# The second expert layer of a two-layer model: three row buffers, the choice of experts one batch sooner, and its biases as one rounded matmul pass over 24 rows

## The reference, cut to what matters

```
scores = maximum((x @ gate_W + gate_b) / 1.0, 1e-4)
p = softmax(scores)
_, topk_idx = top_k(p, 2)
topk_mask = one_hot(topk_idx, 8).sum(-2) > 0
w = maximum(p, 0.1)
w = w / take_along_axis(w, topk_idx).sum(-1)
comb = where(topk_mask, w, 0)
y = einsum('bsd,edf->bsef', x, expert_W) + expert_b
out = einsum('bsef,bse->bsf', y, comb) / 2
```

## Time and profile before

| what | us |
|---|---|
| median of 3 runs (2248.28 to 2251.6) | 2251.52 |
| span of the profiled execution, first to last instruction | 2243.7 |
| start of the last stage's first load | 1951.0 |
| first and last batch's first bias matmul | 1980.35 and 2211.24 |

### The profile page before, as it was taken

One profiled execution on the slowest core, in us unless ns is written; L12 is line 12 of the kernel. 1 busy time (PEld: TensorE's weight loads), 2 busy tenths in 40 slices (PEclk: granted clock), 3 DMA queues, 4 the chain that ended last, 5 costly groups with the idle time before them and its releaser, 6 DMA issues. The chain is left out here.

```text
span 2243.7 us, 32891 instructions
## 1 busy us (share of the span) xinstructions
PE 1923.3 (86%) x9910; PEld 1128.5 (50%) x9910; DVE 1660.0 (74%) x2326; ACT 1242.8 (55%) x2642; POOL 1427.3 (64%) x1164
## 2 busy tenths in 40 slices
PE   2499999999873999956899999999999996579998
PEld 1244444444432999953345454544444442267676
DVE  4478888787734756520999999999999999546554
ACT  1066666676652434326786868686868575223232
POOL 7334445543343444431999999999999999534344
PEclk9789999999875999977999999999999999879899
DMA  3544544444144444421231314040404040200110
GB/s 79 107 98 104 114 106 109 115 110 123 50 154 132 92 72 76 77 45 61 110 123 47 135 36 157 13 161 10 161 10 151 10 158 3 67 11 29 37 37 19
DMA packets 231218, 185.60 MB, mean 83 GB/s; under 512 B 148729, under 2 KB 201601, under 8 KB 231058
## 3 DMA queue, kind: packets, MB, share of 16 engines
q1 hardware_dynamic: 216178, 162.61, 25.1%
q0 software_dynamic: 13296, 17.77, 4.4%
q10 hardware_dynamic: 1584, 3.24, 0.5%
HBM read 134.07 MB, written 49.49 MB: 82 GB/s over the span
## 5 line engine op out<-in xcount | busy, mean ns | idle before, releaser
L1780 POOL TENSOR_TENSOR mb_dbu<-mb_dtu,mb_bbc 128x1024 f32<-128x1024 f32 x256 | 598.6, 2360 | 5.2 <-DVE mb_da_ps L1937 2.4
L473 ACT ACTIVATE ex_plain<-at_t_ps 128x512 f32<-128x512 f32 x512 | 289.4, 595 | 176.1 <-PE at_t_ps L851 170.2
L1937 DVE TENSOR_TENSOR_SCAN mb_da_ps<-mb_da_ps,mb_dbu 128x1024 f32<-128x1024 f32 x160 | 365.3, 2283 | 4.0 <-ACT mb_da_ps L1830 3.3
L1972 PE MATMUL mb_y_ps<-mb_hc,lw_ident 128*128 128x512 f32 x640 | 312.3, 611 | 44.9 <-DVE mb_hc L1944 44.4
L610 DVE TENSOR_REDUCE at_mx<-at_s_ps 128x2 f32<-128x1024 f32 x256 | 310.8, 1218 | 48.3 <-PE at_s_ps L860 45.3
L860 PE MATMUL at_s_ps<-ex_w 48*128 48x512 f32 x512 | 226.1, 503 | 37.5 <-DVE at_mx L610 24.1
L851 PE MATMUL at_t_ps<-ex_w 64*128 64x512 f32 x512 | 219.8, 485 | 12.4 <-ACT ex_plain L473 7.1
L1786 POOL TENSOR_TENSOR mb_hp<-mb_hp,mb_cbc 128x1024 f32<-128x1024 f32 x96 | 226.0, 2354 | 0.0
L1935 DVE TENSOR_TENSOR_SCAN mb_hp<-mb_da_ps,mb_dbu 128x1024 f32<-128x1024 f32 x96 | 218.8, 2280 | 6.5 <-POOL mb_dbu L1780 5.5
L1211 POOL DMA_INDIRECT x<-m_o,m_xs x71 | 113.7, 1601 | 172.7 <-DMA x<-m_o,m_xs 106.3
L1972 PEld LDWEIGHTS mb_y_ps<-mb_hc,lw_ident 128*128 128x128 f32 x640 | 117.7, 192 | 203.7 <-issue 124.5
(11 more groups left out here) (322 smaller groups left out, 4148.1 us busy)
## 6 DMA issues: line engine op xcount, KB each, us to landing
mb_bbc<-mb_scr SPq DMA_DIRECT2D x64, 512.0 KB, 6.2
mb_cbc<-mb_scr SPq DMA_DIRECT2D x64, 512.0 KB, 6.2
ex_w<-at_scr SPq DMA_DIRECT2D x384, 64.0 KB, 2.3
m_xs<-rt_rows SPq DMA_DIRECT2D x71, 129.0 KB, 2.0
at_scr<-at_qk_hi SPq DMA_DIRECT2D x32, 256.0 KB
at_scr<-at_qk_lo SPq DMA_DIRECT2D x32, 256.0 KB
at_xin<-in_x SPq DMA_DIRECT2D x32, 128.0 KB, 2.2
ex_plain<-in_x SPq DMA_DIRECT2D x8, 512.0 KB
```

The costliest lines, as they stand in the source:

```text
L473: act.activation(probs[:, c, h, :], t_ps[:, k % 2, :], ACT.Exp, scale=SCALE).then_inc(exp_done, 1)
L1780: pool.tensor_tensor(dbu[:, q % 3, :, :], dtu_2, bbc[:, 2 * p:2 * p + 2, :], ALU.mult).then_inc(S["dbu_ready"], 1)
L1937: dve.tensor_tensor_scan(da, da, add, 0.0, ALU.mult, ALU.add).then_inc(S["scan_done"], 1)
L1972: last = pe.matmul(y_ps[:, v % 2, :], ident[:, :], src[:, j, :], start=False, stop=(q == tile_last[v] and j == 1))
```

## The change

The four tables of places and the loop over two batches are gone; the eight batches are written out. Rows have three buffers instead of two, so that a batch's rows are there two batches ahead. Variance (and ACT's root) of batch n + 2 is taken at the end of batch n; the other steps for batch n + 1 move forward: normalising after unit 0, turned rows after 3, gate after 6, and on DVE scores after 6, the first choice after 8, the second after 10, the shares after 12. PE turns the shares after unit 14. DVE's instructions for the choice are the same as before.

The bias product becomes one pass of rounded numbers: the shares are split into a rounded part and the rest, and stand three times beside each other (`comb_3`: rounded, rest, rounded) against biases that stand three times below each other (`eb_3`: rounded, rounded, rest), 24 rows in all. This adds three small DVE instructions per batch, and in the prologue four on the biases and one more constant, `parts_of`.

```
-        x = sb("x", [P, 2, 4, D])
+        x = sb("x", [P, XB, 4, D])
...
-        combT = sb("combT", [E, 2, T])
+        comb_3 = sb("comb_3", [P, 4, 3, E], F32R)
+        combT = sb("combT", [3 * E, 2, T], F32R)
...
+                for n in range(NB):
+                    for u in range(UNITS):
+                        if u % 2:
+                            add_odd(n, u)
+                        if u == 7 and n + 1 < NB:
+                            low(n + 1)
...
+                            if u == 3:
+                                take_rows(n + 1)
+                            if u == 7:
+                                exponents(n + 1)
+                            if u == 14:
+                                take_comb(n + 1)
+                        if u == 15 and n + 2 < NB:
+                            root(n + 2)
...
+                    dve.tensor_scalar(comb[:, n % 2, :, :], m1, 0.5, None, ALU.mult).then_inc(S["comb_ready"], 1)
+                    dve.wait_ge(S["comb_ready"], n + 1)
+                    wait(dve, S["combT_ps"], n)
+                    top_steps(dve.tensor_copy(comb_3[:, :, 0, :], comb[:, n % 2, :, :]))
+                    dve.tensor_copy(comb_3[:, :, 2, :], comb_3[:, :, 0, :])
+                    dve.tensor_tensor(comb_3[:, :, 1, :], comb[:, n % 2, :, :], comb_3[:, :, 0, :], ALU.subtract).then_inc(S["comb_3_ready"], 1)
...
+                    for u in range(0, UNITS, 2):
+                        accumulate(n, u)
+                        if n + 1 < NB:
+                            if u == 0:
+                                normalise(n + 1)
+                            if u == 6:
+                                scores(n + 1)
+                            if u == 8:
+                                first_choice(n + 1)
+                            if u == 10:
+                                second_choice(n + 1)
+                            if u == 12:
+                                shares(n + 1)
+                        if u == 14 and n + 2 < NB:
+                            variance(n + 2)
...
+                    wait(pe, S["b_added"], 2 * n + k // 2 - 1)
+                    pe.wait_ge(S["eb_ready"], 4)
+                    for a in range(2):
+                        last = pe.matmul(b_ps[:, k // 2, a * D:(a + 1) * D], combT[:, n % 2, (k + a) * P:(k + a + 1) * P], eb_3[:, :], start=True, stop=True)
...
+                        if n + 1 < NB:
+                            if u == 3:
+                                turn_rows(n + 1)
+                            if u == 6:
+                                gate(n + 1)
+                            if u == 14:
+                                turn_comb(n + 1)
```

More of the change, by code:

```diff
@@ L1439, in _ @@
                 act.preload_act_table_set("natural_log_exp_and_others")
[L1440 to L1464, removed]
@@ L1466, in weigh_odd, with root @@
[L1466 removed]
+                act.wait_ge(S["const_set"], 1)
+                def root(n):
+                    act.wait_ge(S["var_ready"], n + 1)
+                    wait(act, S["xn_ready"], n)
+                    act.activation(rs[:, 0, :], mv[:, :, 1], ACT.Ln, bias=eps[:, :]).then_inc(S["ln_ready"], 1)
+                    act.wait_ge(S["ln_ready"], n + 1)
+                    act.activation(rs[:, 0, :], rs[:, 0, :], ACT.Exp, scale=-0.5).then_inc(S["rs_ready"], 1)
@@ L1496, in slot @@
+                root(0)
+                upper(0)
+                upper(1)
+                take_rows(0)
+                root(1)
+                exponents(0)
+                upper(2)
+                upper(3)
+                take_comb(0)
+                for n in range(NB):
+                    act.wait_ge(S["comb_ready"], n + 1)
                     for u in range(UNITS):
                         if u % 2:
-                            weigh_odd(n, b, u)
-                        if following and u in ACT_AT:
-                            before(*following, ACT_AT.index(u))
@@ new lines, in gate, with turn_comb @@
+                def gate(n):
+                    pe.wait_ge(S["xT_hi_ready"], n + 1)
+                    for k in range(4):
+                        for kt in range(2):
+                            last = pe.matmul(f_ps[:, 0, k * E:(k + 1) * E], xT[:, kt, k * P:(k + 1) * P], gw[:, kt, :], start=(kt == 0), stop=(kt == 1))
+                    last.then_inc(S["logits"], 1)
+                def turn_comb(n):
+                    pe.wait_ge(S["comb_3_ready"], n + 1)
+                    for k in range(4):
+                        last = pe.transpose(f_ps[0:3 * E, 0, k * P:(k + 1) * P], comb_3[:, k, :, :].rearrange("p s e -> p (s e)").bitcast(F32), ident[:, :])
+                    last.then_inc(S["combT_ps"], 1)
@@ new lines, in biases @@
+                def biases(n, k):
+                    wait(pe, S["b_added"], 2 * n + k // 2 - 1)
+                    pe.wait_ge(S["eb_ready"], 4)
+                    for a in range(2):
+                        last = pe.matmul(b_ps[:, k // 2, a * D:(a + 1) * D], combT[:, n % 2, (k + a) * P:(k + a + 1) * P], eb_3[:, :], start=True, stop=True)
+                    last.then_inc(S["b_ready"], 1)
+                turn_rows(0)
+                gate(0)
+                turn_comb(0)
+                for n in range(NB):
+                    pe.wait_ge(S["xT_lo_ready"], n + 1)
+                    pe.wait_ge(S["combT_ready"], n + 1)
```

333 lines of the change are left out of this document (157 added, 176 removed).

## The result

The changed kernel takes 2231.56 us (median of 4 runs, 2228.57 to 2237.41) against 2251.56 for the kernel before: a ratio of 0.992, interval 0.9901 to 0.9939. It is faster, as forecast.

The account below looks back on a forecast made before the run. PE in the last stage was taken to bound the kernel, 33.0 us a batch. Seven batches -12.6, the last -1.5, prologue +3.9 gave -10.2, so 2241.3 us; own range 2235 to 2248, over all cases 2228 to 2254.

Parts of the forecast that it names:

- The waits: PE's stalls per batch: 0.9 for normalised rows after unit 3, 2.7 for shares after unit 14; the shares' copy wait goes.
- The price of `xT_lo` in the choice: On DVE, the first choice waits for POOL's `xT_lo` and the adds behind it: 1.3 us, between 0 and 2.3.
- The work of PE: PE's own work per batch in the last stage, without waits and clock, was to fall to 26.0 us.
- I take half of that, 0.23 for the two, and keep the 0.2: Price of the one-pass bias product on PE: two 256-column matmuls, 0.43 us instead of 1.05 at full clock.
- I therefore keep a fall per batch: Clock term: the granted clock still falls once every batch, the shorter kind, costing 1.6 us; bounds 0 and 3.3.
- The prediction's own sign of being wrong: Over a batch of the last stage, a granted clock of 0.98 or 0.85 would show the forecast wrong.
- the clock that stays up: Rival: in the last stage's batches nothing is lost to the clock, 11.2 us less, 2230; chance 0.16.
- The prologue: Work ahead of the last stage's batches: constant +0.4, `comb_3` behind POOL's weight passes +4.9, bias product -1.4; together +3.9 us.
- the prediction's own row of L1535: In batch 3, the choice's last DVE instruction takes 0.62 us beside POOL's add, elsewhere 0.2: DVE does wait for POOL.
- The 1.4 that the first bias product was to give back: In the prologue sum, the stage's first bias product at low clock gets shorter: 2.04 - 0.6 = 1.4 us.
- The last batch: Batch 7, without a successor: its two bias products of 1.37 and 1.05 become 0.43 each, -1.5 us.
- The median of the runs lies 7.8 above that span, and I let what surrounds it be: Last step: from the traced span's forecast, 2233.5 us, to the median's by keeping the 7.8 difference: 2241.3.

Follow-up runs that it names:

- e3: The changed kernel with POOL's `xT_lo` behind unit 5's add instead of unit 7's; 2221.62 us, ratio 0.9870.
- e2: The kernel before with the one-pass bias product alone, its order and two row buffers kept; 2248.4 us, ratio 0.9994.
- e6: The changed kernel with the constant `parts_of` widened from 2 to 16 columns (2 used), so later buffers start where they would at multiples of 64 bytes; 2236.51 us.
- e9: The changed kernel with choice one pair sooner, `xT_lo` behind unit 5, `parts_of` 16 columns wide, POOL's last weight splits behind `comb_3`; 2205.66 us, ratio 0.9812.
- e4: The kernel before, run again unchanged; 2250.31 us, ratio 1.0004.
- e10: The changed kernel with the choice one pair sooner and 32 unused bytes ahead of `xT_hi` and behind `xT_lo`; 2214.72 us (1 run).
- e11: The changed kernel with the choice one pair sooner, `parts_of` 16 columns wide, and 32 unused bytes putting `xT_hi` and `xT_lo` off; 2212.41 us (1 run).
- e12: The changed kernel without the one-pass bias, choice one pair sooner, `xT_lo` behind unit 5, `xT_hi` and `xT_lo` 32 bytes off; 2220.7 us (1 run).

## Why the prediction was right, step by step

The period was forecast as 31.2 and measured as 31.15, and that closeness is luck: against the kernel before, PE's work was to fall by 1.7 and fell by 0.6, the waits were to grow by 1.1 and grew by 0.7, the clock was to give 1.2 and gave 2.0.

- **The waits** moved where they were forecast: for the shares behind unit 14 (2.7 said, 2.92 measured), for the rows after unit 3 (0.9 said, 0.44 measured), none for `combT`. The price of `xT_lo` in the choice, 1.3, was right for the first choice (1.1, and 0.25 for the add behind it); e3 shows 1.8 in all, with the hits in the second choice that follow from the delay. POOL's hits came to 2.8 where some 1.7 lay in the sum, DVE's own work to 8.4 where it had 8.9, and PE's six units to 8.4 where it had 8.0.
- **The work of PE was taken too low**, 26.0 for 27.1. "I take half of that, 0.23 for the two, and keep the 0.2" gave 0.43, and the chain's row for the product alone is 0.43. But the product starts 0.32 behind the matmul ahead and the second matmul behind it 0.34 behind the first, where units have 0.23 from one to the next: 0.2 more per product. Turned rows that PE has to wait for take 1.09 and not 0.87. And 96 matmuls at 0.004 more add 0.4: no term foresaw that a small buffer moves the ones behind it.
- **The clock was taken too high.** "I therefore keep a fall per batch" is the step that failed: the clock fell at two borders of seven in one execution of this kernel, at three in the other. The prediction's own sign of being wrong, a granted clock of 0.98 over a batch, came in five of seven batches (0.99 and four times 1.00). Its rival, the clock that stays up, was thus half true: 5.4 and 7.9 of the low clock were left where the forecast had 11.2 and the rival nothing. Idle time goes with falls: before and in e2, where PE stands idle for 2.3 to 3.6 at a border, in two pieces, the clock fell at all seven borders; in the changed kernel and e6, where it is 2.0 to 3.0 in one piece, at two, three and five of seven; in the eight kernels where it is 1.8 or less, at none. But after the same 2.92 it fell at some borders and not at others, so the length of the wait alone does not decide; what else does stays open.
- **The prologue was taken too dear.** The first bias product came 2.8 later; the sum had 0.4 + 4.9 = 5.3. The three instructions of `comb_3` cost 2.5 of it and not 4.9. The Trainium skill ("SBUF — State Buffer", section "SBUF: two separate sides") has a copy wait for POOL if it runs in a two-port mode. The trace agrees that a copy with a single SBUF input waits, 2.20 instead of 0.18, but for one pass and not for both; which mode it ran in no row shows. That a single SBUF input is enough stood already in the prediction's own row of L1535, 0.62 beside POOL's add. Normalising did wait for both passes; why the subtraction got in between them stays open. That e9 takes the 2.2 back shows the cause: its prologue differs in POOL's order and the wide constant, and e6, with the wide constant alone, keeps 32.3 to the first bias product. The constants (+0.3) and the work put under the 7.74 of idle time cost what was said.
- **Two terms at the ends.** The 1.4 that the first bias product was to give back was counted twice at least in part: the first of the seven periods starts with that product, so 0.6 of it lay in the -12.6 already. The last batch gave 2.5 and not 1.5, for the fall of the clock at its border went too.
- **From the span to the median** is the step that failed most. "The median of the runs lies 7.8 above that span, and I let what surrounds it be": what surrounds a span is 1.7 to 2.0 in every traced execution that has its own time (2231.6 - 2229.8; 2248.96 - 2247.2 in e4). The other 6 were luck of the one traced execution of before. With 1.8 the same sum gives 2235.3. Of the 9.7 by which the forecast missed, 6.0 are this step, 2.35 the stage, and 1.35 that the stages ahead ended sooner in the traced execution of after.
- **Left open:** the stage became 12 us shorter in the traces (292.7 and 294.5 before, 280.2 and 282.6 after), the medians differ by 16 to 20. The stages ahead, whose code is unchanged, end between 1949.65 and 1955.84 in the traces, so single executions can't settle the rest of what the medians show.

## What to carry to other kernels

When one engine waits for another, look at what a change puts on the late one and at what then runs beside it: here the bias pass saved PE 1.2 a batch and cost DVE 1.8, most of it not in its three instructions but in POOL's passes, which now met the choice. The pass paid only when the choice was moved out of PE's way (e9). Count the low clock as a term of its own: it was most of the gain. Put POOL's long passes where DVE has nothing with two SBUF inputs to do. And after adding a small buffer, look at where the buffers behind it start.

## What the runs showed of the hardware

- Rounded matmuls of 512 columns start 0.2333 us apart when the rows that PE loads (`xT_hi`, `xT_lo`) start 32 bytes off a multiple of 64, and 0.228 to 0.229 when they start at one (11.41 against 11.12 to 11.22 for 48). Moving those two buffers alone by 32 bytes switches it, both ways (e10, e11, e12). Why kernels with the rows at a multiple of 64 differ among themselves, 11.12 and 11.22, stays open.
- A DVE copy of 128x32 with a single SBUF input waited 2.0 us for a POOL pass, like instructions with two, and the next instruction came in between two POOL passes of one list (0.18).
- The same program with the same waits (2.92, and 2.03 or 2.04 once) saw the granted clock fall from 1.00 to 0.50, the levels of 2.4 and 1.2 GHz, at two borders of seven in one execution and at three in another.
